# FFN stage: the next group's context steps moved up by one expert, and two of them into the end of the rounds

## What is computed

```python
x = x + _L0_xattn_ref(_layernorm(x, axis=-1), ctx_1024, ...)   # slots against 1500 context tokens
x = x + _L0_ffn_ref(_layernorm(x, axis=-1), router_w, w1, w2)  # 8 experts, top 2

# _L0_xattn_ref(slots, P, ...)
Pn = rmsnorm(P, input_norm_w)
k_proj = Pn @ Wk.T
v_proj = Pn @ Wv.T
for _ in range(3):
    sn = rmsnorm(slots, slot_norm_w)
    q_proj = sn @ Wq.T
    scores = einsum('bkd,bmd->bkm', q_proj, k_proj) * SCALE
    attn = softmax(scores, axis=-2)
    attn = attn / (sum(attn, axis=-1, keepdims=True) + EPS)
    slots = gru_cell(einsum('bkm,bmd->bkd', attn, v_proj), slots, ...)

# _L0_ffn_ref, for each of 8 experts
h = gelu(x_flat @ w1[eid].T)
out = out + w[:, None] * (h @ w2[eid].T)
```

## Time and profile before

| | us |
|---|---|
| median of 3 runs | 780.38 (779.99 to 782.31) |
| the profiled execution | 780.16 |
| its span, first to last instruction | 777.6 |
| DVE busy | 660.0 (85%) |
| PE busy | 615.5 (79%) |
| POOL busy | 512.2 (66%) |
| ACT busy | 495.0 (64%) |
| DVE's share of the chain that ended last | 48% |
| PE's share of it | 20% |

### The profile page before, as it was taken

How to read it: one execution, slowest core, us unless ns; L and a number is a source line. 1 busy time by engine, 2 the same in 40 slices (tenths; PEclk the granted TensorE clock), 3 DMA queues, 4 the chain that set the end, 5 groups by cost and what they waited for, 6 DMA issues and landing times.

```text
span 777.6 us, 28408 instructions
## 1 busy us (share of the span) xinstructions
PE 615.5 (79%) x12300; PEld 531.2 (68%) x12300; DVE 660.0 (85%) x1370; ACT 495.0 (64%) x964; POOL 512.2 (66%) x434
## 2 busy tenths in 40 slices
PE   2566699986868699995777789996677779998697
PEld 1455699974545699984455689996355579997475
DVE  4777799995999889996899789998699779998565
ACT  3666366764877457764878456765786637765475
POOL 5984478887566278888467278888495458888000
PEclk9876899996898799998978889999798879999799
DMA  9673300000876900000487630000197600000000
GB/s 190 145 193 97 82 3 4 5 3 13 161 162 121 209 8 5 3 4 13 98 183 149 145 84 4 4 5 2 42 212 161 116 22 4 4 4 4 1 1 13
DMA packets 89927, 52.04 MB, mean 67 GB/s; under 512 B 75907, under 2 KB 84755, under 8 KB 89803
## 3 DMA queue, kind: packets, MB, share of 16 engines
q1 hardware_dynamic: 89803, 50.23, 30.1%
HBM read 30.29 MB, written 0.92 MB: 40 GB/s over the span
## 4 chain that ended last, share of the span: by engine, by line
DVE 48%; PE 20%; issue 14%; ACT 8%; POOL 6%; DMA 3%; SPq 1%; POOLq 0%; DVEq 0%; ACTq 0%
DVE score_ps L1039 8%; PE score_ps L509 6%; DVE inv_sum L1078 5%; DVE ctx_rows L887 5%; DVE soft L1057 5%; DVE top L1032 5%; DVE hidden L1100 3%; DVE ssq L883 3%; DVE rden L1075 2%; PE upd_ps L496 2%; POOL ctx_raw L791 2%; PE score_ps L496 2%; PE upd_ps L462 2%; DVE upd L1081 2%; DVE npre L1046 2%
## 5 line engine op out<-in xcount | busy, mean ns | idle before, releaser
L854 POOL TENSOR_TENSOR soft<-soft,rden 125x672 f32<-125x672 f32 x96 | 126.1, 1314 | 59.4 <-DVE rden L1075 59.2
L848 POOL TENSOR_TENSOR attn<-soft,attn 125x672 f16<-125x672 f32 x96 | 140.6, 1465 | 35.9 <-ACT attn L719 35.5
L509 PEld LDWEIGHTS score_ps<-w_t,hidden 128*128 128x128 f16 x1536 | 102.2, 105 | 88.7 <-DVE hidden L1100 74.2
L509 PE MATMUL score_ps<-w_t,hidden 128*128 128x128 f16 x1536 | 117.7, 232 | 51.7 <-DVE hidden L1100 51.1
L449 PE MATMUL score_ps<-qk,ctx_cols 128*128 128x56 f16 x3456 | 112.3, 192 | 8.8 <-DVE rden L1075 6.4
L462 PE MATMUL upd_ps<-attn,ctx_rows 126*128 126x56 f16 x3456 | 108.3, 189 | 11.8 <-POOL attn L848 11.5
L462 PEld LDWEIGHTS upd_ps<-attn,ctx_rows 126*128 126x128 f16 x3456 | 105.5, 97 | 14.3 <-POOL attn L848 13.9
L449 PEld LDWEIGHTS score_ps<-qk,ctx_cols 128*128 128x128 f16 x3456 | 103.9, 99 | 9.7 <-issue 9.0
L791 POOL TENSOR_TENSOR ctx_raw<-ctx_raw,ctx_rstd 125x1536 f32<-125x1536 f32 x32 | 101.2, 3163 | 2.5
L719 ACT CAST attn<-soft 125x672 f16<-125x672 f32 x96 | 71.6, 746 | 43.5 <-POOL soft L854 43.5
L733 ACT ACTIVATE soft<-soft 125x672 f32<-125x672 f32 x96 | 73.2, 762 | 40.0 <-DVE soft L1057 39.5
(11 more groups left out here) (144 smaller groups left out, 1186.0 us busy)
## 6 DMA issues: line engine op xcount, KB each, us to landing
ctx_raw<-in_ctx_dram SPq DMA_DIRECT2D x32, 672.0 KB
soft<-in_L_ffn_w_dram SPq DMA_DIRECT2D x16, 256.0 KB, 4.9
ctx_raw<-in_ctx_dram SPq DMA_DIRECT2D x32, 78.0 KB
x_in<-in_x_dram SPq DMA_DIRECT2D x4, 224.0 KB, 2.6
out_dram<-acc SPq DMA_DIRECT2D x4, 224.0 KB, 2.9
ctx_cols<-ctx_rows SPq DMA_TRANSPOSE x24, 7.4
soft<-in_L_xattn_gru_wih_dram SPq DMA_DIRECT2D x1, 192.0 KB, 3.8
soft<-in_L_xattn_gru_whh_dram SPq DMA_DIRECT2D x1, 192.0 KB, 4.4
```

The source lines that it names most:

```text
L509: mm = pe.matmul(score_ps[:, 2 + e % 2, t * D:(t + 1) * D], hidden[:, n % HRING, hp, t * ROWS:t * ROWS + D], w2_t[:, wp, e, c * D:(c + 1) ...
L848: nc.gpsimd.tensor_tensor(attn[0:TP, s % 3, LO], soft[0:TP, s % 4], attn[0:TP, s % 3, HI], ALU.subtract).then_inc(attn_ready, 1)
L854: nc.gpsimd.tensor_tensor(a, a, rden[0:TP, s % 2].unsqueeze(2).to_broadcast([TP, CHUNKS, SLOTS]), ALU.mult).then_inc(soft_ready, 1)
```

## The change

Every context step of the FFN stage stands one expert earlier, and the steps for which there is no earlier expert stand before the loop. `rows_hi` of context 0 and `square_ctx` of context 2 (`EARLY`) come on ACT behind the last round, ahead of the copy of the FFN input. `rows_lo` of context 0 comes on DVE behind the router's probabilities. In the loop, expert e now has `sum_squares(e+2)` at c = 1 (before, the sum of e+1 at c = 0), `rows_hi(e+1)` at c = 2, `square_ctx(e+3)` and `rows_lo(e+1)` at c = 3. Between the sum of a context and its high half there are five chunks and not six. On POOL `rstd_rows` follows context 3 and not 2; `first_rstd_h` keeps its place. PE and SP have the same order as before.

```diff
--- before.py
+++ after.py
@@ -736,6 +736,9 @@
                         square_ctx(i + 1, early_at(n + 1))
                     if m is not None:
                         qk_hi(i, m)
+                if more:
+                    rows_hi(i + 1, 0)
+                    square_ctx(i + 1, EARLY)
                 copy_cols(ycols[:, :], score_ps[:, 3], nth(i, LNT_PER, ln_tile(RT - 1)))
                 nc.scalar.copy(ycols16[:, HI, :], score_ps[:, 3, 0:PW]).then_inc(y_hi_ready, 1)
                 wait(act, router_shift, nth(i, 1, 1))
@@ -753,10 +756,10 @@
                         hid_hi(n - 1)
                     e, c = divmod(n, HC)
                     if more:
-                        if c == 3 and EARLY <= e + 2 < PAIR:
-                            square_ctx(i + 1, e + 2)
-                        if c == 2:
-                            rows_hi(i + 1, e)
+                        if c == 2 and e + 1 < PAIR:
+                            rows_hi(i + 1, e + 1)
+                        if c == 3 and e + EARLY + 1 < PAIR:
+                            square_ctx(i + 1, e + EARLY + 1)
                         if n == 4 * HC + 3:
                             copy_cols(hflat, gru_ps[:, 1], nth(i + 1, LNT_PER, RT))
                         if n == QUERIES_AT - 1:
@@ -863,7 +866,7 @@
                         scale_ctx(i + 1, e)
                         if e == EXPERTS - 2:
                             first_rstd_h(i + 1)
-                        if e == 2:
+                        if e == 3:
                             rstd_rows(nth(i + 1, LNT_PER, RT))
 
             for i in range(NPAIR):
@@ -1092,6 +1095,8 @@
                 nc.vector.tensor_tensor(ycols16[:, LO, :], ycols[:, :], ycols16[:, HI, :], ALU.subtract)\
                     .then_inc(y_split, 1)
                 router_probs(i)
+                if more:
+                    rows_lo(i + 1, 0)
                 for n in range(CH + HC):
                     e, c = divmod(n, HC)
                     if 1 <= n <= CH:
@@ -1115,10 +1120,10 @@
                                 scalar=mix[:, t, e - 1:e], in1=acc[:, t, :], op0=ALU.mult, op1=ALU.add)
                         ins.then_inc(mixed, 1)
                     if more:
-                        if EARLY <= e + 1 < PAIR and c == 0:
-                            sum_squares(i + 1, e + 1)
-                        if e < PAIR and c == 3:
-                            rows_lo(i + 1, e)
+                        if e + EARLY < PAIR and c == 1:
+                            sum_squares(i + 1, e + EARLY)
+                        if e + 1 < PAIR and c == 3:
+                            rows_lo(i + 1, e + 1)
                         if n == HC + 3:
                             wait(dve, x_loaded, nth(i + 1, DMA, DMA))
                             row_stats(x_in)
```

## The result

The changed kernel takes 788.37 us in the median of 10 runs (785.12 to 791.92), the one before 780.65 beside it (776.82 to 784.81). The ratio is 1.0100, with a 95% interval of 1.0072 to 1.0129: slower by 7.7 us in the medians, where 793.5 us and a range of 779 to 801 had been forecast. The profiled execution of the changed kernel took 789.92 us with a span of 787.8, so the two traces differ by 10.2 us of span, more than the medians do. I compare the traces by stage, and the kernels by their runs. Ratios leave out the one run of the whole set that was in the slow state, a run with L910 at chunk 12.

A forecast was written before the change was run, and what follows sets the result against it. No engine was full; waits between engines, DVE and POOL blocking each other and three raw buffers counted. Terms -5.8 + 2.9 - 2.4 + 3.2 + 4.2 + 2.4 gave +4.5 us a stage, +13.5 in three: 793.5 us, range 779 to 801.

The forecast's parts named there:

- a new stand of ACT and PE at `rows_hi(7)`: Late in each stage ACT waits 4 us for POOL at `rows_hi(7)`, with DVE and PE behind; part of +3.2 us.
- a tie at `rows_lo(1)`: DVE against POOL's multiply, 0.05 us apart, POOL taken as first; worth 2.5 us a stage at most.
- a longer drain: After `rows_lo(7)`: eight chunks' worth of `hidden` and not four, 9.1 us against 4.9, +4.2 us a stage.
- the clock: TensorE falls to half rate after long waits: 0 to 4.8 us a stage, the middle of 2.4 taken.
- the last contexts: Contexts 6 and 7: POOL's L812 (2.52 us) delays context 7; `square(7)` to `rows_lo(7)` 20.3 us against 17.1, +3.2 us.
- context 1 and 2: `square(3)` to `square(4)` takes 10.3 us against 7.39, with POOL's multiply ahead of `rows_lo(1)`: +2.9 us a stage.
- One blocked `rows_lo` in the middle remains of three: Contexts 3 to 7: `rows_lo(4)` is blocked to 409.0; the steps between squares give -2.4 us together.
- The start: Start of the stage: `rows_lo(0)` ahead of chunk 0 lets load 3 issue sooner; `square(3)` at 379.45, not 385.25: -5.8 us.
- No change: Rival: DVE wins at `rows_lo(1)` in each stage (-2.5), TensorE's rate costs no more than before (-2.4); 779 to 780, chance 0.09.
- The faster one: Rival: raw buffers started 5.8 us sooner and freer `rows_lo` carry the stage, POOL's chain hidden; total 773, chance 0.15.
- The worse one: Rival: DVE waits over 0.6 us for ACT before `rows_lo`, POOL first each time, two more blocked a stage; 803, chance 0.1.

The follow-up runs named there:

- the run with the start alone: The kernel before with only `rows_hi(0)` and `square(2)` ahead of the FFN input copy and `rows_lo(0)` behind the router's probabilities; 777.92 us, ratio 0.9961.
- the first experiment: The changed kernel with `rows_lo(1)` one step earlier on DVE, ahead of `mix_weights`, in each FFN stage with contexts; 785.44 us, ratio 1.0061.

## Why the prediction was right, and where it was not

**The direction and the mechanism** held: slower, by a new stand of ACT and PE at `rows_hi(7)` behind L815 in every stage, by a tie at `rows_lo(1)` that POOL wins (0.05 us, as walked), and by a longer drain. The sum by term, for the second stage, in us from ACT's copy of the FFN input (367.56 before, 371.31 after); measured are the starts in the rows above and in the same view:

| step | forecast | measured |
|---|---|---|
| `square(3)` | 11.9 | 11.9 |
| `square(4)` | 22.2 | 22.5 |
| `square(5)` | 28.7 | 29.5 |
| `square(6)` | 37.2 | 37.4 |
| `square(7)` | 47.0 | 47.4 |
| `rows_hi(7)` | 63.3 | 62.3 |
| `rows_lo(7)` | 67.3 | 66.3 |
| end of the last `acc` | 76.4, and 2.4 for the clock | 77.0 |

**A price that was off** is in the last contexts. I took 2.52 us for L812 from the earlier trace rows. L815 takes 1.01, as the rows above have it. The 2.52 was no price of the step: in the kernel before it started at 422.34 inside `rows_lo(5)`, which ran from 420.20 to 423.99, and was held by DVE as DVE is held by POOL. From `rows_hi(6)` to `rows_hi(7)` I had 9.7 us and it was 8.2; the 1.5 us between are the part of L812's price that was a hold. ACT's wait at `rows_hi(7)` was 2.5 us, not 4, and `rows_lo(7)` came 1.0 us sooner than walked.

**The sum over three stages**, term by term, changed less before, in us:

| term | forecast | measured |
|---|---|---|
| start, up to `square(3)` | -17.4 | -16.8 |
| `square(3)` to `square(4)` | +8.7 | +11.2 |
| `square(4)` to `square(7)` | -7.2 | -8.4 |
| `square(7)` to `rows_lo(7)` | +9.6 | +7.9 |
| `rows_lo(7)` to the end, with the clock | +19.8 | +17.6 |
| together | +13.5 | +11.5 |

Each term has the sign that was forecast, and the sum is near because errors of both signs partly cancel: context 1 and 2 cost more, the last contexts and the drain less. The spans differ by 10.2 us. The medians differ by 7.7, where 13.1 had been forecast; the profiled execution of the changed kernel is 1.6 us above its median, and single runs scatter (776.8 to 784.8 for the kernel before). So by the medians the size came out at six tenths of the forecast. Of that gap of 5.4 us the traces account for 2.0 in these stages and 1.3 in the rest of the kernel.

**Blocked steps.** "One blocked `rows_lo` in the middle remains of three" held in number in the second and third stage and not in place. I had walked it for `rows_lo(4)`; of contexts 2 to 7 it is `rows_lo(5)` that is long in all three stages (4.29 to 4.30 us), by a tie of 0.07 us. At chunk 15 one of two is held each time: `rows_lo(4)` in the first stage (4.22 us), so that two remain there, and L910 in the other two. I had not seen that L910 can be held. The squares came on time all the same, since `square(7)` hangs on `rows_lo(4)`, and in two of three stages that was free.

**The start** was given as -5.8 us for `square(3)`, and that it was in the second stage (-6.7 and -4.3 in the others). Its worth by itself is 2.8 us in three stages: in the run with the start alone, by `square(4)` only 1.8 to 1.9 us of it are left in two of them and 1.1 in the third, and the blocked steps behind it are all there.

**The clock.** I gave it 2.4 us in a stage. In the tail of the changed kernel, behind the pause of 3.21 us ahead of L424, the granted clock falls:

```profile
438.00:442.00 4.00, 4.00 (x36) 3.06 (x35) 2.54 (x3) 2.37 (x6) 0.00 (x0) 0.66 0.39 74
```

The last part, from `rows_lo(7)` to the end, takes 10.7 us and not 9.1. Other runs with the same order there show what the clock has in this: with `first_rstd_h` behind context 7 the part takes 9.34 us in the first stage, at a granted clock of 1.00, and 10.71 in the second, at 0.84. Against 9.34 the three stages of the changed kernel (10.46, 10.71 and 11.89) lost 5.1 us together, where I had 7.2 for the whole clock term. What the clock did elsewhere in the stage no run here takes apart. The Trainium skill's page on it (TensorE: Matmul & The Clock Gate, HAM oscillation) would have put the total some 7 us higher; the stages' mean clock of 0.83 to 0.86 against 0.84 to 0.87 before says that this did not happen. The kernel before had a fall of this kind too, so not each fall in the changed kernel is an added one.

**The rivals.** *No change* needed the tie to go to DVE, and it went to POOL in all three stages; where the first experiment gave it to DVE, the kernel was still at 785.44. The faster one (773) asked for a distance of `rows_hi(6)` to `rows_hi(7)` of over 9.6 us without a wait. It was 8.2 us with 2.5 of wait in it. The worse one needed DVE to be late for every `rows_lo`; it was in one or two places a stage only, the multiply of context 6 each time and that of context 5 in the first stage.

## What to carry to other kernels

When a chain of steps is shifted against a loop, list the steps that were not shifted and wait for a step of the loop; here POOL's 1 us for the queries stood in front of a context that was now three chunks sooner, and cost 17 us in one order and 4 in another. A chain that ends earlier in a loop also leaves more of the loop behind it, here 5 to 6 us a stage, and must first win that back. A recorded duration can hold the wait for another engine; compare it with the same step where nothing runs beside it before it enters a sum. And where two engines exclude each other, give the cheap one a lead that it keeps, for a tie of 0.05 us costs 2.5; 0.18 us was enough for `rows_lo(1)` in the kernel before. Then look at what stands behind the cheap step, for the hold may only move there, as it did to L1022.

## What was not expected of the hardware

POOL's small power step is held by DVE in the same way as its multiply (2.55 and 2.52 us for 1.01), and DVE's TENSOR_SCALAR from SBUF (L910, four steps of 112x128 f32, 3.54 for 1.10) is held by POOL, while the low half of `hidden` from PSUM stays near 0.62 us beside it. A TENSOR_TENSOR of 112x32 elements (L1011, L1022) took 2.75 and 2.74 us for 0.19 and 0.18. So DVE and POOL do not meet only at semaphores, as I had written of the engines. The Trainium skill (SBUF — State Buffer, SBUF: two separate sides) says that the shared port pair is an exclusive lock, which the one that starts first keeps for the whole instruction; the trace agrees, to 0.05 us (383.62 against 383.67), and in the run with the start alone for the other order (383.70 against 383.75).
